# Pyramid-pooled attention: the last batch convolved in pairs, its attention in one piece behind them

## The reference

```
qk    = relu(bn(conv1x1(x, qk_w)))            # x: 8 x 512 x 64 x 64, qk: 256 channels
val   = relu(bn(conv1x1(x, v_w)))             # 512 channels
key   = psp(qk); value = psp(val)^T           # max pooling to 1 + 9 + 36 + 64 = 110 cells
query = qk as 4096 positions x 256 channels
p     = softmax(query . key / 16)             # over the 110 cells
y     = p . value                             # 4096 x 512
out   = x + bn(conv1x1(y, out_w))
```

## Time and profile before

| | us |
|---|---|
| three runs | 1298.03, 1299.38, 1303.01 (median 1299.38) |
| the profiled execution | 1298.87, its span 1297.1 |
| busy: PE, DVE, ACT, POOL | 1282.8, 951.6, 688.9, 953.3 |
| granted TensorE clock | 0.998 of full speed in the mean |

### The profile page before, as it was taken

The page is one execution under the profiler, slowest core; times in us unless marked ns, Lnnn a source line. Parts: engine busy times, 40 slices in busy tenths (PEclk is TensorE's granted clock), DMA queues, the critical chain, the costliest instruction groups (busy, mean ns, idle before and its releaser), DMA issues.

```text
span 1297.1 us, 16867 instructions
## 1 busy us (share of the span) xinstructions
PE 1282.8 (99%) x5561; PEld 1038.8 (80%) x5561; DVE 951.6 (73%) x2171; ACT 688.9 (53%) x1017; POOL 953.3 (73%) x414
## 2 busy tenths in 40 slices
PE   9999999999999999999999999999999999999997
PEld 7788788887888878887888878888788887878885
DVE  6666777777777768778677787777877778886576
ACT  5334655654455654455654466654555637664422
POOL 2998988786788777888777887877877835765532
PEclk9999999999999999999999999999999999999999
DMA  6323357666667657666566676656676669995426
GB/s 228 114 98 114 130 179 244 204 198 215 212 226 244 211 164 232 222 226 232 182 204 229 224 244 195 201 205 230 208 239 213 201 215 354 348 311 187 154 98 259
DMA packets 134537, 272.20 MB, mean 210 GB/s; under 512 B 9226, under 2 KB 9266, under 8 KB 134450
## 3 DMA queue, kind: packets, MB, share of 16 engines
q1 hardware_dynamic: 134162, 270.59, 61.9%
q10 hardware_dynamic: 288, 0.52, 0.1%
HBM read 174.61 MB, written 96.47 MB: 209 GB/s over the span
## 4 chain that ended last, share of the span: by engine, by line
PE 85%; DVE 7%; ACT 3%; POOL 3%; issue 2%; DMA 1%; DVEq 0%; ACTq 0%; POOLq 0%
PE conv_ps L727 18%; PE conv_ps L734 18%; PE conv_ps L729 18%; PE out_ps L818 4%; PE out_ps L819 4%; PE out_ps L820 4%; PE conv_ps L711 3%; PE conv_ps L710 3%; PE conv_ps L709 3%; PE score_ps L781 2%; PE score_ps L780 2%; PE score_ps L782 2%; POOL xl L608 1%; DVE row_max L1402 1%; PE sum_ps L790 1%
## 5 line engine op out<-in xcount | busy, mean ns | idle before, releaser
L1402 DVE TENSOR_REDUCE row_max<-conv_ps 128x64 f32<-128x384 f32 (+2 forms) x575 | 283.9, 529 | 131.1 <-ACT q_out L1089 68.3
L608 POOL TENSOR_TENSOR xl<-xa,xh 128x1024 fp32r<-128x1024 f32 x106 | 254.2, 2427 | 85.6 <-ACT xh L1018 85.6
L727 PE MATMUL conv_ps<-xh,sh 128*128 128x512 f32 x646 | 253.6, 393 | 0.8 <-DVE conv_ps L1465 0.8
L729 PE MATMUL conv_ps<-xh,sl 128*128 128x512 f32 x646 | 253.0, 392 | 0.0
L608 POOL TENSOR_TENSOR xl<-tt,xh 128x1024 fp32r<-128x1024 f32 x81 | 195.3, 2428 | 17.0 <-ACT xh L1018 17.0
L734 PE MATMUL conv_ps<-xl,sh 128*128 128x512 f32 x646 | 200.7, 392 | 0.7 <-POOL xl L608 0.7
L727 PE MATMUL conv_ps<-xh,wh 128*128 128x512 f32 x474 | 186.2, 393 | 0.8
L729 PE MATMUL conv_ps<-xh,wl 128*128 128x512 f32 x474 | 185.3, 391 | 0.0
L1026 ACT ACTIVATE conv_ps<-conv_ps 128x512 f32<-128x512 f32 x81 | 47.2, 583 | 245.8 <-PE conv_ps L734 245.1
L1542 DVE SCALAR_TENSOR_TENSOR xo<-out_ps,shift,xo 128x512 f32<-128x512 f32 x205 | 151.9, 746 | 33.0 <-DMA xo<-x 16.8
L633 POOL TENSOR_TENSOR q_l<-q_in,q_h 128x1024 fp32r<-128x1024 f32 x50 | 120.7, 2415 | 74.6 <-ACT q_h L1098 74.6
(11 more groups left out here) (270 smaller groups left out, 2537.1 us busy)
## 6 DMA issues: line engine op xcount, KB each, us to landing
xa<-x SPq DMA_DIRECT2D x148, 512.0 KB, 6.0
xo<-x SPq DMA_DIRECT2D x104, 512.0 KB, 4.3
out<-xo SPq DMA_DIRECT2D x104, 512.0 KB, 3.7
queries<-q_out SPq DMA_DIRECT2D x112, 256.0 KB, 2.9
q_in<-queries SPq DMA_DIRECT2D x50, 512.0 KB, 4.1
tt<-x SPq DMA_DIRECT2D x13, 512.0 KB, 5.5
out<-tt SPq DMA_DIRECT2D x13, 512.0 KB, 4.2
early<-queries SPq DMA_DIRECT2D x6, 512.0 KB, 7.3
```

The costliest lines, as they stand in the source:

```text
L608: nc.gpsimd.tensor_tensor(lo[:, :, :], PARTS[i][0], hi[:, :, :], ALU.subtract).then_inc(x_lo, 1)
L727: nc.tensor.matmul(out[:, :], hi[:, k, :], x_hi_part[:, k, :], start=start and k == 0, stop=False, skip_group_check=True)
L729: nc.tensor.matmul(out[:, :], lo[:, k, :], x_hi_part[:, k, :], start=False, stop=False, skip_group_check=True)
L1402: last = nc.vector.tensor_reduce(row_max[:, c, n, :], src[:, r0_ * W:r1_ * W].rearrange("p (r w) -> p w r", w=W), AX.X, ALU.max)
```

## The change

All 32 pairs (`PAIRS = S // 2`) are convolved by `pair_product`; the direct convolution of batch 7, its second load of x and its places for queries in SBUF go. Its queries are spilled to DRAM and loaded into buffers that come free in the last pair (`q_in`, `tt`, parts of `xh` and `xl`). In the last pair some operations stand elsewhere in the queues: the scores of its second attention tile earlier, `finish_values` ahead of its exponentials, refine and normalise ahead of the last row maxima. Behind the pairs the rest of batch 6's attention follows, then batch 7's, two tiles deep: scores(a + 2), projections of a, sums(a + 2). The residual x of the last nine tiles is loaded into freed buffers, and the ring of `xo` has two buffers for all other tiles. Lines in brackets describe removed code.

```diff
-    PAIRS = LAST // 2
+    PAIRS = S // 2
-    queries = nc.dram_tensor("queries", [LAST, P, QC, TN], F32).ap()
+    queries = nc.dram_tensor("queries", [S, P, QC, TN], F32).ap()
...
         def q_from(a):
-            if a >= LAST:
-                return q_place(a)
-            k = early_place(a)
-            return q_in[:, :, :] if k is None else early[k][:, :, :]
+            if a <= LAST:
+                return q_in[:, :, :]
+            i = a - LAST - 1
+            if i < 3:
+                return tt[:, i, :, :]
+            _, b0, b1 = PARTS[5 + (i - 3) // 2]
+            return [xh_free, xl_free][(i - 3) % 2][:, b0:b1, :]
...
         def score_bank(a):
-            return conv_ps[3] if a >= LAST - NT and a % 2 else score_ps
+            return conv_ps[3] if a >= LAST and a % 2 else score_ps
         def pv_bank(k):
-            return conv_ps[3] if k == B - 2 else out_ps[1]
-        LAST_BANKS = [out_ps[0], *conv_ps[0:3], out_ps[1], score_ps]
+            return conv_ps[2] if k == B - 1 else out_ps[1]
+        LAST_BANKS = [conv_ps[0], conv_ps[1], out_ps[0], out_ps[1], conv_ps[2]]
...
@@ GpSimd, behind the pairs
-            (tiles s = LAST .. S + NT - 1: two split_lo of x, one split_q_lo each)
+            for a in range(LAST, LAST + 3):
+                split_q_lo(a)
             for a in range(LAST, S - 1):
                 add_copy(a)
+                if a + 3 < S:
+                    split_q_lo(a + 3)
...
@@ TensorE, the last pair (s == PAIRS - 1)
+                    pair_product(s, 0, lambda: sums(B0), lambda: project(A - 2, 2),
+                                 lambda: project(A - 2, 3), lambda: project(B0, 0))
+                    pair_product(s, 1, lambda: scores(A), lambda: (sums(A), project(B0, 1)),
+                                 lambda: project(B0, 2), nothing)
+                    pair_product(s, 2, lambda: (project(B0, 3), scores(A + 1)), nothing,
+                                 lambda: (sums(A + 1), project(A, 0)), lambda: project(A, 1))
@@ TensorE, behind the pairs
-            (s = LAST .. S - 1: conv(s, 4), conv(s, 5) between the attention of batch 6;
-             s = S .. S + NT - 1: conv(s, 0..3) between scores and sums of batch 7)
-            (project_values, scores(S - 1), all projections of batch 7)
+            projections((LAST - 2, 2), (LAST - 2, 3))
+            for m in range(VC):
                 project_values(B - 1, m)
+            projections(*((LAST - 1, m) for m in range(OC)))
+            scores(LAST)
+            sums(LAST)
+            scores(LAST + 1)
+            sums(LAST + 1)
             for a in range(LAST, S):
+                if a + 2 < S:
+                    scores(a + 2)
+                projections(*((a, m) for m in range(OC)))
+                if a + 2 < S:
+                    sums(a + 2)
...
@@ ScalarE, in the last pair
-                    split_hi(LAST, 1)
+                    finish_values(B - 1)
                 if A >= 0:
                     exps(A + 1)
...
                 store_pair_q(s, 2)
                 if nxt:
                     split_part_hi(nxt, 6)
+                else:
+                    guess(A + 1)
                 store_pair_q(s, 3)
+            split_p_hi(LAST - 1)
+            split_q_hi(LAST)
+            finish_keys(B - 1)
             values_hi(B - 1)
+            for a in (LAST, LAST + 1):
+                exps(a)
+                split_q_hi(a + 1)
+                guess(a)
+                split_p_hi(a)
+            for a in range(LAST + 2, S):
+                exps(a)
+                if a + 1 < S:
+                    split_q_hi(a + 1)
+                copy_out(a - 2)
+                guess(a)
+                split_p_hi(a)
+            copy_out(S - 2)
...
@@ VectorE, in the last pair
                 make_u4(s, 2)
+                if s == PAIRS - 1:
+                    finish_grids(0, VC, values_pooled)
...
                 pool_pair_rows(s, 2, 2)
+                if s == PAIRS - 1:
+                    cell_values_lo(B - 1)
+                    refine(A + 1)
+                    normalise(A + 1)
+                    add_out(A, 1)
+                    pool_cells(t0 + 1, VC, CC, pair_group(s, 2) + 3)
                 pool_pair_rows(s, 2, 3)
@@ VectorE, behind the pairs
+            pool_cells(NT - 2, VC, CC, GROUPS)
+            finish_grids(VC, CC, keys_pooled)
+            split_p_lo(LAST - 1)
+            add_out(LAST - 2, 2)
+            add_out(LAST - 2, 3)
+            keys_lo(B - 1)
+            for m in range(OC):
+                add_out(LAST - 1, m)
+            values_lo(B - 1)
+            split_e_lo(LAST)
+            refine(LAST)
+            normalise(LAST)
+            split_e_lo(LAST + 1)
+            split_p_lo(LAST)
+            refine(LAST + 1)
+            normalise(LAST + 1)
+            add_out(LAST, 0)
+            split_p_lo(LAST + 1)
+            for a in range(LAST, S):
+                if a + 2 < S:
+                    split_e_lo(a + 2)
+                for m in range(1, OC):
                     if not copied(a, m):
                         add_out(a, m)
+                if a + 2 < S:
+                    refine(a + 2)
+                    normalise(a + 2)
+                if a + 1 < S:
+                    add_out(a + 1, 0)
+                if a + 2 < S:
+                    split_p_lo(a + 2)
```

More of the change, by code:

```diff
@@ L127, in psp_attention @@
         s_raw1 = over("s_raw1", [P, 4, HALF, P], "e_l")
-        spare_h = over("spare_h", [P, 3, 2, TN], "xh", 8 * TN)
-        spare_l = over("spare_l", [P, 3, 2, TN], "xl", 8 * TN)
-        early = [over(f"early{i}", [P, QC, TN], "sh" if i < 2 else "sl", (1 + 2 * (i % 2)) * TN) for i in range(4)]
+        xh_free = over("xh_free", [P, 14, TN], "xh")
+        xl_free = over("xl_free", [P, 14, TN], "xl")
         conv_ps = [psum(f"conv_ps{i}") for i in range(4)]
@@ L528, in _ @@
                     store(2 * A - 2)
+                if s == PAIRS - 1:
+                    for a in range(LAST + 1, LAST + 4):
+                        load_q(a)
+                    for h in range(RING, RING + 4):
+                        load_residual(h)
                 if A + 2 >= 0:
@@ L898, in _ @@
                                  lambda: project(A, 1))
+                elif s == PAIRS - 1:
+                    pair_product(s, 0,
+                                 lambda: sums(B0),
+                                 lambda: project(A - 2, 2),
+                                 lambda: project(A - 2, 3),
+                                 lambda: project(B0, 0))
+                    pair_product(s, 1,
+                                 lambda: scores(A),
+                                 lambda: (sums(A), project(B0, 1)),
+                                 lambda: project(B0, 2),
+                                 nothing)
+                    pair_product(s, 2,
+                                 lambda: (project(B0, 3), scores(A + 1)),
+                                 nothing,
+                                 lambda: (sums(A + 1), project(A, 0)),
+                                 lambda: project(A, 1))
                 else:
@@ L1761, in _ @@
-            add_outs(LAST + 1)
-            add_outs(LAST + 2)
-            refine(S - 1)
-            add_outs(LAST + 3)
-            normalise(S - 1)
-            add_outs(LAST + 4)
-            split_p_lo(S - 1)
-            for a in range(LAST + 5, S):
-                add_outs(a)
+                if a + 2 < S:
[5 more added lines that the diff above has]
+                    split_p_lo(a + 2)
```

484 lines of the change are left out of this document (95 added, 389 removed).

## The result

The changed kernel takes 1332.45 us in the median (1331.19 to 1336.28, four executions) against 1299.2 of the kernel before: ratio 1.0256 [1.0225, 1.0286]. Predicted were 1318 and a range up to 1332. The direction was right, the size was 14.5 us short and just outside the range.

A forecast was written before the change was run, and what follows sets the result against it. The prediction took back-to-back matmuls on TensorE to bound the kernel. Its terms summed to 246.55 us from 1069.7, a span of 1316.3; with 1.8 between span and time it forecast 1318 us, range 1305 to 1332.

The forecast's parts named there:

- first two tiles: Start of batch 7's attention: 6.92 us for each tile, 13.85 together, since `exps(57)` stands behind `split_p_hi(56)` on ScalarE.
- last exponent to last add's end: End of the tail, from `exps(63)` through p's low part and four projections to the last add: 12.5 us.
- stores: After the last add, the same four stores follow each other: 5.5 us, bounds 4.2 and 6.
- Pairs 28 to 31: Paired convolution replaces direct convolution: 72 matmuls fewer, 16.6 us saved, with extra spills and query loads priced at nothing.
- The handover: From pair 31's last `u1_done` to batch 7's first exponent: 20.35 us; counted from pair 31's start, 53.15.
- 4 us for waits that I missed: Upper allowance on the 20.35 us between pair 31's last `u1_done` and the first exponent of batch 7.
- The ring: Batch 7's tail from `exps(58)` on: a loop through ScalarE, GpSimd and TensorE, 8.28 us a tile, five steps, 41.4 us.
- rival 4: Tail: GpSimd isn't in the ring, 7.7 us a step, time 1315, or 1311 with a shorter handover; chance 0.15.
- The clock: Tail: TensorE idles 3.2 us five times, and falls to half clock cost 2 us, bounds 0 and 14.
- Rival 3: Tail: the clock falls in the ring and stays low, adding 14 us, time 1330; chance 0.14.
- Rival 1: Tail: it runs at VectorE's rate, 5.25 us for each of seven steps, time 1298, no change; chance 0.05.
- rival 2: Tail: attention at TensorE's 4.65 us a tile with a handover of 13.7, time 1287, faster; chance 0.04.

The follow-up runs named there:

- e10_spill_apart: The changed kernel with the last pair's first three spills ahead of the eight residual loads and GpSimd's first sum waiting for VectorE's four weight scalings: 1320.49 us, 1.0155.
- e3_warm: The changed kernel with eight dummy matmuls ahead of the scores of each of tiles 57 to 63: 1328.48 us, ratio 1.0226.
- e2_qfirst: The changed kernel with GpSimd taking the query's low part ahead of `add_copy` in the tail: 1328.16 us, ratio 1.0227.
- e11_no_warm: e9_keys_alone without the eight dummy matmuls ahead of the scores of tile 56: 1293.88 us, ratio 0.9964 to the kernel before.
- e9_keys_alone: e8_pipe_apart with GpSimd's split of tile 57's query held until the low part of the last keys is written: 1294.77 us, ratio 0.996.
- e8_pipe_apart: The changed kernel with a reordered handover and tail, split queries in four buffers, eight dummy matmuls before tile 56, GpSimd's first sum held until VectorE's scalings end: 1296.71 us, 0.9977.

## Why the prediction was wrong

The profiled span is 1334.6, predicted 1316.3. By the prediction's own steps the 18.3 us are:

| step | predicted | measured | difference |
|---|---|---|---|
| up to pair 28 | as before | 4.50 late | + 4.5 |
| pairs 28 to 30 | 118.15 | 118.15 | 0 |
| pair 31's start to the exponent of tile 56 | 53.15 | 66.9 | + 13.7 |
| first two tiles | 13.85 | 15.2 | + 1.35 |
| ring, five steps | 41.4 | 43.1 | + 1.7 |
| last exponent to last add's end | 12.5 | 12.3 | - 0.2 |
| stores | 5.5 | 4.7 | - 0.8 |
| clock, priced apart | 2 | in the rows above | - 2 |

**Pairs 28 to 31: right.** 41.6 and three times 38.27, no idle TensorE, 72 matmuls fewer.

**The handover: here the prediction failed**, in a sentence of the part on the pairs: "So I price this at nothing; the queries are loaded into buffers that come free in pair 31, at least 10 us before the tail wants them". I had compared the mean DMA share of the stretch, 0.71, and asked only whether the loads come in time. I had not walked SyncE's queue in the last pair, and so missed that the spills, whose landing frees `q_out` for a store on the path, stand behind eight residual loads of 0.5 MB, and these behind a load that itself waits 10.1 us for a store to land. Behind that store now follow the last row maxima, cells and keys. What the runs show in its place: the fourth query's store waits 15.45 us, and the handover takes 66.9 us instead of 53.15. `e10_spill_apart` shows the cause: with three spills put ahead of the eight loads and the clash at the start taken out, the exponent of tile 56 comes 0.6 us from the forecast, and 12.9 of the 13.7 us are back. The bound of "4 us for waits that I missed" was a third of what was missed.

**The ring: right in mechanism and size.** 8.25 to 8.28 a tile at full clock (`e3_warm`), GpSimd in it (`e2_qfirst`), which is why rival 4 fell.

**The clock: the mechanism right, its size some 3 for 2.** It fell and rose again (0.50 from 1270.45 to 1277.28, 1.00 from there to 1290.93, 0.50 to 1294.35), which made the mean of the window from 1259 to 1318 0.86. The first two tiles, 15.2 us for 13.85, are where it shows besides the ring: with the dummies they are 14.15. Rival 3, a clock that stays low, would have been 14 and fell, although its time, 1330, is near to the measured one: its number was right for a wrong reason. The Trainium skill ("TensorE: Matmul & The Clock Gate", part 1, "HAM oscillation") describes how the rate falls in the waits between bursts of matmuls, burst after burst, and the trace agrees that such falls occur (the stretches at 0.50 above). The price here was small, since most of the ring is ScalarE's, VectorE's and GpSimd's.

**The late start: not foreseeable from one trace,** but 1303.01 among three times at 1298 and 1299 was a hint that some executions have it. In the median it counts less than in the profile: the two lower executions of the changed kernel are at 1331.2 and 1331.4, so if these are free of the clash, it explains about 1.2 us of the median's error of 14.5; the handover is nearly all of it.

**What the change was worth.** The saving of 16.6 us of matmuls was real, and `e11_no_warm` gets 4.6 of it. Rival 1 and rival 2 described what a better order does; the written order was what kept them away, as the prediction said.

Left open: how the late start is distributed over executions (too few were run), what makes the clock fall in some executions of the deeper tail, and whether `e11_no_warm` is faster than `e9_keys_alone` in the median, which the ratios don't settle. A split of VectorE's tail work (some of its adds to ScalarE and GpSimd) wasn't tried.

## What to carry to other kernels

When work that an engine used to cover moves onto the path, walk *every* queue that feeds it, SyncE's line by line: a store into a rotating buffer waits for the landing of a DMA that may be queued behind megabytes of others. A mean DMA share says nothing about the order in one pair. A dependent chain that is now bare needs its depth counted in tiles, and after each cure the next wait must be looked for, the cure itself among the suspects.

## What the runs showed of the hardware

GpSimd slows some of VectorE's operations between SBUF tensors far more than I had expected: four scalings 1.67 us alone, 8.04 and 10.15 beside GpSimd; `value_l` 0.61 and 2.14; `key_l` 0.39 and 2.40. GpSimd's own low part of a query takes 2.36 us beside them and 2.35 without. In `e8_pipe_apart` each slowed subtraction ends just behind GpSimd's operation beside it: 1233.00 behind 1232.52, 1235.97 behind 1235.73. VectorE's operations with an operand in PSUM are not slowed beside it; timeline of VectorE and GpSimd in `e8_pipe_apart`:

```profile
1242.78 0.70 DVE L1371 SCALAR_TENSOR_TENSOR sum_ps<-sum_ps,r 128x512 f32<-128x512 f32 x1 [2.04 <-ACT r L1054]
...
1240.94 2.41 POOL L599 TENSOR_TENSOR wl<-tt,wh 128x1024 fp32r<-128x1024 f32 x1 [5.22 <-ACT wh L1002]
```

The Trainium skill ("GPSIMD Engine Reference", 1. Specifications) says that GpSimd shares its SBUF interfaces with VectorE and contends with instructions in a 2-port mode or with two inputs in SBUF. The runs agree for two inputs in SBUF (`key_l`, `value_l`) and add the size. The scalings read one SBUF tensor and are slowed too; that they run in a 2-port mode no trace here says. In all profiles together, from 1070 us on, the refinement shown above takes 0.70 us beside GpSimd (109 times) and 0.69 without (85 times), and the maxima from `row_max` to `cells` (128x256 to 128x16), which read one SBUF tensor, take 0.41 us either way. The second surprise: such a stall at 28 us of the kernel starved TensorE for 3 us and shifted all that followed by 4.5 us, to the end.
